# Latent attention: maxima and exponentials of opposite row halves sent to TensorE in turn, head groups in order 0,1,2,3

## The reference

```python
x + attn(xn) + ffn(xn)
# attn: 16 heads of width 8 within chunks of 16 tokens, once on the tokens in order,
#       once on every third token; both outputs summed, then a linear layer
# ffn:  y = xn + mla(rmsnorm(xn));  y + moe(rmsnorm(y))
# mla:
scores = einsum("bqhd,bkhd->bhqk", qq, kk) / sqrt(8)      # 16 heads of width 8, half of it rotated
probs  = softmax(where(tril(ones(S, S)), scores, min))    # causal, S = 512
y      = einsum("bhqk,bkhd->bqhd", probs, v) @ W_o
# moe:  one shared expert and 2 of 7 routed ones per token; all 8 are computed for every token
```

## Time and profile before

| | us |
|---|---|
| median of 3 runs | 514.09 |
| lowest and highest | 512.26, 516.3 |
| the profiled execution, its own time | 514.96 |
| its span, first to last instruction | 513.0 |
| mean granted TensorE clock | 0.963 of full |
| TensorE busy | 464.1 (90%) |
| VectorE busy | 361.0 (70%) |
| ScalarE busy | 265.1 (52%) |

### The profile page before, as it was taken

One profiled execution on the slowest core, in us unless ns is written; L12 is line 12 of the kernel. 1 busy time (PEld: TensorE's weight loads), 2 busy tenths in 40 slices (PEclk: granted clock), 3 DMA queues, 4 the chain that ended last, 5 costly groups with the idle time before them and its releaser, 6 DMA issues.

```text
span 513.0 us, 11641 instructions
## 1 busy us (share of the span) xinstructions
PE 464.1 (90%) x4428; PEld 244.8 (48%) x4428; DVE 361.0 (70%) x1049; ACT 265.1 (52%) x486; POOL 53.2 (10%) x52
## 2 busy tenths in 40 slices
PE   3774988999999999999999997999999999987995
PEld 2322343445453555545455554454545545654652
DVE  6463586687767877776577784666677775688886
ACT  6252447457766554877754385776543444212110
POOL 4231001141001121010002120000010000010000
PEclk9868699999999999999999997999999999999899
DMA  6156000156000227100001264000400000000000
GB/s 206 24 137 116 0 3 2 21 127 134 3 2 3 65 56 134 27 3 2 2 3 34 54 125 68 1 3 2 125 1 4 2 1 22 0 22 1 1 20 21
DMA packets 18198, 20.22 MB, mean 39 GB/s; under 512 B 2824, under 2 KB 16392, under 8 KB 17352
## 3 DMA queue, kind: packets, MB, share of 16 engines
q1 hardware_dynamic: 18144, 19.49, 17.4%
HBM read 10.84 MB, written 7.47 MB: 36 GB/s over the span
## 4 chain that ended last, share of the span: by engine, by line
PE 60%; DVE 20%; DMA 6%; issue 5%; ACT 5%; SPq 3%; POOL 1%; DVEq 0%; ACTq 0%; POOLq 0%
PE bank_A L1080 7%; PE bank_c L1043 6%; PE bank_A L1001 6%; PE bank_B L1026 6%; PE bank_M L1091 6%; DVE x L942 4%; PE bank_B L1124 4%; DMA q_stack<-in_c_rows 4%; PE bank_M L1098 4%; DVE k_diag L922 3%; PE bank_B L1031 3%; PE bank_M L985 3%; DVE k_diag L927 3%; PE bank_A L1130 2%; SPq L478 2%
## 5 line engine op out<-in xcount | busy, mean ns | idle before, releaser
L672 ACT ACTIVATE p_mla<-bank_B 128x512 f32<-128x512 f32 (+1 forms) x176 | 97.5, 561 | 92.9 <-PE bank_B L1031 91.4
L819 DVE CUSTOM_DVE_ANT_0 differences<-masks,bank_A 128x384 bf16<-128x384 bf16 (+1 forms) x128 | 78.4, 613 | 25.2 <-PE bank_A L1001 20.2
L651 ACT ACTIVATE pT_loc<-sT_loc 32x512 f32<-32x512 f32 x136 | 85.1, 625 | 4.8 <-DVE sT_loc L845 3.4
L1001 PE MATMUL bank_A<-k_stack,q_stack 50*128 50x128 bf16 (+3 forms) x256 | 65.2, 307 | 11.0 <-DMA q_stack<-in_c_rows 7.4
L1124 PE MATMUL bank_B<-xrT,k_diag 128*128 128x512 f32 x128 | 64.4, 617 | 3.9 <-DVE k_diag L922 3.2
L1026 PE MATMUL bank_B<-q_stack,k_stack 50*128 50x512 bf16 (+3 forms) x256 | 63.9, 302 | 0.6 <-DVE k_diag L922 0.2
L838 DVE TENSOR_REDUCE row_max<-bank_A 128x16 f32<-128x512 f32 (+1 forms) x36 | 24.8, 690 | 40.7 <-PE bank_A L1080 40.6
L1080 PE MATMUL bank_A<-k_diag,qT 128*32 128x512 f32 x272 | 50.5, 772 | 0.0
L1031 PE MATMUL bank_B<-masks 64*128 64x64 bf16 (+1 forms) x512 | 50.3, 202 | 0.0
L1043 PE MATMUL bank_c<-p_mla,v_mla 128*9 128x128 f32 (+3 forms) x512 | 47.5, 442 | 0.4 <-ACT p_mla L672 0.3
L1031 PEld LDWEIGHTS bank_B<-masks 64*128 64x128 bf16 x512 | 39.8, 95 | 14.3 <-issue 0.2
(11 more groups left out here) (135 smaller groups left out, 593.3 us busy)
## 6 DMA issues: line engine op xcount, KB each, us to landing
parts_dram<-parts SPq DMA_DIRECT2D x16, 192.0 KB, 2.7
k_stack<-parts_dram SPq DMA_DIRECT2D x8, 384.0 KB
q_stack<-parts_dram SPq DMA_DIRECT2D x8, 384.0 KB
parts_dram<-parts SPq DMA_DIRECT2D x16, 128.0 KB, 2.7
k_diag<-kT SPq DMA_DIRECT2D x64, 18.0 KB
x<-in_x SPq DMA_DIRECT2D x4, 256.0 KB, 6.6
parts_dram<-parts SPq DMA_DIRECT2D x16, 64.0 KB, 2.3
out<-x SPq DMA_DIRECT2D x4, 256.0 KB, 2.2
```

The costliest lines, as they stand in the source:

```text
L651: last = nc.scalar.activation(pT_loc[rows, :, rows], sT_loc[rows, t % 2, :].rearrange("p (h k) -> p h k", h=H), ACT.Exp, scale=SCALE)
L672: drained_by(nc.scalar.activation(p_mla[:, n % P_RING, m:m + len(heads), j * P:], src, ACT.Exp, scale=SCALE), step)
L819: drained_by(nc.vector.tensor_tensor_reduce(differences[:, 0:w], masked16[:, S - w:], bank[:, 0:w], -1.0, -NEG, ALU.add, ALU.min, dst), step)
L1001: last = nc.tensor.matmul(bank[:, n * w:(n + 1) * w], q_stack[b % 2][rows, h % 8, i * P:(i + 1) * P], k_stack[b % 2][rows, h % 8, 0:w], st ...
```

## The change

`GROUP_ORDER` becomes 0, 1, 2, 3. The lists "maxima" and "latent" of all batches give way to one list "scores" from key -0.29 to 4.0, made of 18 slots of 11 elements (`LEAD` = 2). In slot n an element holds an S step of group n (counted through all batches) and the E step of the same place of group n-2, then what is due behind it (PV of the key block that has just ended; SHIFT of the group before, behind the second element). The first two slots hold S alone, the last two E alone. An element is placed as a whole, so nothing stands between its S and its E. The units of S come in the order i = 3, 2, 1, 0, which gives the two steps of an element equal numbers of matmuls of equal width. TensorE issues such a pair in turn: first matmul of E, first of S, second of E, second of S, and then the masks of E with those of S in turn, where S has any. The stretches of the outputs and of the norm of batches 1 and 2 move slightly. No operation is added or removed on any engine.

```diff
@@ -77,14 +77,15 @@
 LOCAL_TILES = S // P
 
 
-GROUP_ORDER = [0, 2, 1, 3]
+GROUP_ORDER = [0, 1, 2, 3]
+LEAD = 2
 
 
 def score_units():
 
     units = []
     for g in GROUP_ORDER:
-        for i in range(NT):
+        for i in reversed(range(NT)):
             n = S // ((i + 1) * P)
             units += [(i, list(range(h, min(h + n, 4 * g + 4)))) for h in range(4 * g, 4 * g + 4, n)]
     return units
@@ -103,14 +104,13 @@
 
 
 SPREAD = {
-    "latent": [(0, 1.12), (1.12, 2.02), (2.02, 2.86), (2.86, 4)],
-    "maxima": [(-0.29, 0.63), (0.61, 1.44), (1.56, 2.46), (2.49, 3.54)],
+    "scores": [(-0.29, 4.0)],
     "local": [(-0.53, 0.39), (0.36, 1.22), (1.34, 2.21), (2.28, 3.15)],
     "project": [(0.01, 0.29), (0.35, 1.13), (1.49, 2.32)],
     "stacks": [(-0.37, -0.37), (0.48, 0.48), (1.3, 1.3), (2.29, 2.29)],
     "values": [(-1.27, -1.27), (0.38, 0.38), (1.36, 1.36), (2.34, 2.34)],
-    "outputs": [(1.18, 1.34), (2.12, 2.26), (2.86, 2.97), (4.02, 4.27)],
-    "norm": [(1.31, 1.53), (2.33, 2.54), (3.17, 3.65), (4.28, 4.57)],
+    "outputs": [(1.18, 1.34), (2.13, 2.26), (3.08, 3.19), (4.02, 4.27)],
+    "norm": [(1.31, 1.53), (2.33, 2.54), (3.26, 3.65), (4.28, 4.57)],
     "experts": [(3.17, 5.49)],
     "statistics": [(-0.41, -0.41)],
 }
@@ -120,7 +120,7 @@
 
     keyed = [(lo + (hi - lo) * (k + 0.5) / len(one), n, k, step)
              for n, (one, lo, hi) in enumerate(parts) for k, step in enumerate(one)]
-    return [x[3] for x in sorted(keyed, key=lambda x: x[:3])]
+    return [step for x in sorted(keyed, key=lambda x: x[:3]) for step in (x[3] if isinstance(x[3], list) else [x[3]])]
 
 
 def plan():
@@ -129,20 +129,27 @@
         return [("LN", b), ("XT", b, 0), ("LK", b), ("LQ", b), ("XT", b, 1), ("MA", b, 0), ("MB", b, 0),
                 ("MA", b, 1), ("MB", b, 1)]
 
-    def maxima(b):
-        steps = []
-        for n, g in enumerate(GROUP_ORDER):
-            steps += [("S", b, u) for u in range(PER_GROUP * n, PER_GROUP * n + PER_GROUP)] + [("SHIFT", b, g)]
-        return steps
-
-    def latent(b):
-        steps, late = [], []
-        for g in GROUP_ORDER:
-            for j in range(NT):
-                units = [("E", b, g, j, u) for u in range(len(exp_units(g, j)))]
-                steps += units[:1] + late + units[1:]
-                late = [("PV", b, g, j)]
-        return steps + late
+    def scores():
+
+
+        groups = [(b, g) for b in range(B) for g in GROUP_ORDER]
+        found, shift, late = [], [], []
+        for n in range(len(groups) + LEAD):
+            here = groups[n] if n < len(groups) else None
+            back = groups[n - LEAD] if n >= LEAD else None
+            exps = [("E",) + back + (j, u) for j in range(NT) for u in range(len(exp_units(back[1], j)))] if back else []
+            for k in range(PER_GROUP):
+                unit = []
+                if here:
+                    unit.append(("S", here[0], PER_GROUP * GROUP_ORDER.index(here[1]) + k))
+                if back:
+                    unit.append(exps[k])
+                found.append(unit + late + (shift if k == 1 else []))
+                late = []
+                if back and (k + 1 == PER_GROUP or exps[k + 1][3] != exps[k][3]):
+                    late = [("PV",) + exps[k][1:4]]
+            shift = [("SHIFT",) + here] if here else []
+        return found + [late]
 
     def outputs(b):
         return [("Y", b, i) for i in range(NT)] + [("YT", b), ("X1", b)]
@@ -173,9 +180,9 @@
     steps = first[:4] + [("KD", 0), ("WF",)] + first[4:]
     at = SPREAD
 
-    lists = [(experts(range(B)), *at["experts"][0])]
+    lists = [(experts(range(B)), *at["experts"][0]), (scores(), *at["scores"][0])]
     for b in range(B):
-        lists += [(latent(b), *at["latent"][b]), (maxima(b), *at["maxima"][b]), (local(b), *at["local"][b]),
+        lists += [(local(b), *at["local"][b]),
                   (outputs(b), *at["outputs"][b]), (norm(b), *at["norm"][b]), ([("ST", b)], *at["stacks"][b]),
                   ([("MV", b)], *at["values"][b])]
     for b in range(1, B):
@@ -259,6 +266,8 @@
     gu_no, down_no = numbers(steps, {"GU"}), numbers(steps, {"DOWN"})
     single = [step for step in steps if step[0] == "S" and UNITS[step[2]][0] >= 2]
     downs = [step for step in steps if step[0] == "DOWN"]
+    beside = {e: s for s, e in zip(steps, steps[1:]) if (s[0], e[0]) == ("S", "E")}
+    waits_for_e = set(beside.values())
 
     with ExitStack() as ctx:
         def sb(name, shape, dt=F32):
@@ -950,6 +959,41 @@
             pe.wait_ge(set_up, 1)
             pe.wait_ge(eye_in, 16)
 
+            def half_of(h):
+                return slice(SLOT * (h // 8), SLOT * (h // 8) + SLOT)
+
+            def maxima_matmul(step, n):
+                b, (i, heads) = step[1], UNITS[step[2]]
+                h, w = heads[n], (i + 1) * P
+                rows = slice(half_of(h).start, half_of(h).start + STACK_ROWS)
+                return nc.tensor.matmul(bank_of(step)[:, n * w:(n + 1) * w],
+                                        q_stack[b % 2][rows, h % 8, i * P:(i + 1) * P],
+                                        k_stack[b % 2][rows, h % 8, 0:w], start=n == 0, stop=i >= 2,
+                                        skip_group_check=True)
+
+            def maxima_mask(step, n, low):
+                i, heads = UNITS[step[2]]
+                w = (i + 1) * P
+                return nc.tensor.matmul(bank_of(step)[:, (n + 1) * w - P + low * SLOT:(n + 1) * w],
+                                        half_eye[half_of(heads[n]), low, :],
+                                        half_causal[half_of(heads[n]), low, low * SLOT:], start=False, stop=True,
+                                        skip_group_check=True)
+
+            def exp_matmul(step, m):
+                _, b, g, j, u = step
+                h, w = exp_units(g, j)[u][m], S - j * P
+                rows = slice(half_of(h).start, half_of(h).start + STACK_ROWS)
+                nc.tensor.matmul(bank_of(step)[:, m * w:(m + 1) * w], k_stack[b % 2][rows, h % 8, j * P:(j + 1) * P],
+                                 q_stack[b % 2][rows, h % 8, j * P:], start=m == 0, stop=False, skip_group_check=True)
+
+            def exp_mask(step, m, low):
+                _, b, g, j, u = step
+                w = S - j * P
+                return nc.tensor.matmul(bank_of(step)[:, m * w:m * w + SLOT * (low + 1)],
+                                        half_eye[half_of(4 * g), low, :],
+                                        half_causalT[half_of(4 * g), low, 0:SLOT * (low + 1)],
+                                        start=False, stop=True, skip_group_check=True)
+
             for _ in range(6):
                 nc.tensor.matmul(bank_c[:, 0:P], eye[:], eye[:], start=True, stop=True)
             for step in steps:
@@ -990,25 +1034,17 @@
                                                 start=True, stop=True)
                     full_by(last, step)
                 elif kind == "S":
-                    i, heads = UNITS[step[2]]
-                    w = (i + 1) * P
                     if step[2] == 0:
                         pe.wait_ge(k_ones_in[b % 2], 16 * 2)
                         pe.wait_ge(stacks_in, STACK_IN * (b + 1))
-                    half_rows = slice(SLOT * (heads[0] // 8), SLOT * (heads[0] // 8) + SLOT)
-                    rows = slice(half_rows.start, half_rows.start + STACK_ROWS)
-                    for n, h in enumerate(heads):
-                        last = nc.tensor.matmul(bank[:, n * w:(n + 1) * w],
-                                                q_stack[b % 2][rows, h % 8, i * P:(i + 1) * P],
-                                                k_stack[b % 2][rows, h % 8, 0:w], start=n == 0, stop=i >= 2,
-                                                skip_group_check=True)
-                    for n in range(len(heads) if i < 2 else 0):
-                        for low in range(2):
-                            c = (n + 1) * w - P + low * SLOT
-                            last = nc.tensor.matmul(bank[:, c:(n + 1) * w], half_eye[half_rows, low, :],
-                                                    half_causal[half_rows, low, low * SLOT:], start=False, stop=True,
-                                                    skip_group_check=True)
-                    full_by(last, step)
+                    if step not in waits_for_e:
+                        for n in range(len(UNITS[step[2]][1])):
+                            last = maxima_matmul(step, n)
+                        if UNITS[step[2]][0] < 2:
+                            for n in range(len(UNITS[step[2]][1])):
+                                for low in range(2):
+                                    last = maxima_mask(step, n, low)
+                        full_by(last, step)
                 elif kind == "SHIFT":
                     g = step[2]
                     wait_drained(pe, ("S", b, PER_GROUP * (GROUP_ORDER.index(g) + 1) - 1))
@@ -1017,21 +1053,23 @@
```

(24 more changed lines are left out.)

## The result

The changed kernel takes 550.6 us (median of 4 runs, 545.8 to 553.5) against 515.2; the ratio is 1.067, 95% interval 1.057 to 1.078. The forecast was 487.

What follows compares the result with a forecast made beforehand. TensorE's instruction stream from 75 to 437 us was taken as the bound. Scores 33 us shorter, less 2, times 0.83 gives 26, plus 2.6 from loads makes 28; 514.96 - 28 = 487 us, range 480 to 494.

Steps and rivals of the forecast that it cites:

- The masks: Small mask matmuls of j=2 and j=3 pairs, two halves in turn: 2.5 us lost, if 0.030 us per start were the floor 4.5.
- The stream: TensorE's score steps: 84 us with pairs overlapped in opposite row halves, against 117 before, 33 us less.
- the 2.6 us for the loads: The wait of 2.58 us at 315.57 us, where S of the last batch waits for its loads, is gone.
- the masks or the order would not overlap at all: Two rivals: masks not overlapped, 524 us; no overlap from the order at all, 520 us; chance 0.09 together.
- (9): From 75 to 437 us TensorE's stream gets some 31 us shorter; 0.83 comes through, as VectorE only rises to 78%.
- (5): E starts 18 us later, so some 10 E steps move to a fuller stretch: costs 0 to 3 us, taken as 2.
- (8): E now also waits for the bank of its S before either starts: price nothing to 3 us.
- (7): SHIFT issued two pairs into the next group; SP's queue holds nothing that waits later than before: cost nothing.
- (2): Reversed i matches S and E in columns and number of matmuls, so a pair costs its E: 49.6 us paired.
- The clock: Around no change, chance 0.05: late loads or a lower granted clock somewhere in the new order eat the gain.
- TensorE waits for VectorE's banks of ring A by tens of us: Sign that would show the forecast wrong: TensorE held up by tens of us for the PSUM banks that S uses.
- VectorE or the hand-over takes half: Rival: VectorE's load or the two-bank rings let only half of the 31 us through, 499 us; chance 0.20.

Runs made afterwards that it cites:

- same_half: The changed kernel with group order 0,2,1,3, so both steps of a pair lie in the same row half and can't overlap: 585.5 us, ratio 1.141.
- unalternated: The changed kernel with its list as it is, but TensorE issues all matmuls of S, then all of E: 551.9 us, ratio 1.065.
- a3b2: The changed kernel with three PSUM banks in ring A (S, local scores) and two in ring B (E): 533.6 us, ratio 1.036.
- short_max_after: The changed kernel with VectorE's maxima of i=2 and i=3 taken over the last 128 columns alone: 530.1 us, ratio 1.027.
- gapped: The changed kernel with the slots of its single list following the old stretches of S, with gaps between them: 538.9 us, ratio 1.036.
- stretch_e: Kernel before with group order 0,1,2,3 and i reversed, plus E, PV, outputs and norm in the change's stretches: 523.3 us, ratio 1.017.
- experts_later: The changed kernel with the experts' list starting at key 3.45 instead of 3.17, its end as before: 539.0 us, ratio 1.046.
- scores_early: The changed kernel with the scores' list ending at key 3.8 instead of 4.0, outputs moved with it: 540.8 us, ratio 1.047.
- stretch_s: Kernel before with group order 0,1,2,3 and i reversed, plus S steps in the change's uniform stretches, E staying: 542.1 us, ratio 1.053.
- reversed_alone: The kernel before with i from 3 to 0 and nothing else, group order left at 0,2,1,3: 525.4 us, ratio 1.016.
- order_alone: The kernel before with its lists kept, only group order 0,1,2,3 and i from 3 to 0: 512.2 us, ratio 0.986.

## Why the prediction was wrong

**Right.** The cost of steps and runs (176 runs of half-array steps, 175 forecast). The overlap of opposite halves in all four kinds of pairs. The masks: forecast 2.5 us of loss, measured none, 0.021 us per start. The stream: 33 us shorter by forecast, about 40 by the account above. Also right: the 2.6 us for the loads, gone. Of the rivals, that the masks or the order would not overlap at all can be dropped; so can the sum's upper bound from weight loads one behind the other.

**The step that failed is (9), with (5) and (8) under it:** that of 31 us of shorter stream 0.83 comes through, because VectorE was at 71% and TensorE had hardly a wait. It took the few waits of the kernel before as a property of the engines' loads. They were a property of the list. The new list, at an equal stream, costs 70 us (same_half against before). I priced the new list's placement of S and E against all other work at 2 us (5), and a late bank at 0 to 3 (8); measured, TensorE's waits for p_mla, neg_max, scratch and shift rose from 8 to 44 us. And the last 12 us of shorter stream, those of the alternation, brought 1.3 (unalternated against the change).

How the list does it, as far as the runs show: S without gaps meets VectorE's blocks (the 4.2 us wait behind PICK; a3b2, short_max_after and gapped each give 12 to 20 us back); E late and dense beside the experts (stretch_e 11 us, experts_later 12, scores_early 10). No run relieves ScalarE, whose p_mla is the longest cause of waits (10.3 us, 12.9 in a3b2); its part stays open. In (7) I held that nothing in SP's queue could delay a SHIFT; a SHIFT does stand behind the stacks' loads for 10 us, and for 6.2 already in the kernel before. It decides nothing in the change, only in stretch_s.

**A second failed step: the reversal of i at nothing** (2). I looked only at how sizes match on TensorE. In the old lists it costs 8 us, by a lower clock at equal work and equal idle time; in the new list, nothing that can be measured. Why the clock falls is open.

**The clock** was in the forecast, together with late loads, as a risk of 5 in 100, and by the account it takes 30 us. Mostly it goes with waits: TensorE idles, the clock falls to 1.2 GHz, and the steps behind the wait run slower too. From 212 to 222 us the changed kernel runs at 1.2 GHz throughout, after waits of 0.65 and 1.05 us that end at 209.7 and 211.8 us:

```profile
212.00:222.00 10.00, 9.53 (x52) 4.27 (x52) 4.18 (x11) 5.04 (x10) 0.00 (x0) 0.50 0.01 3
```

But reversed_alone has such a stretch of 20 us with hardly a wait before it, so waits are not the whole of it. Where the forecast named a sign of error, "TensorE waits for VectorE's banks of ring A by tens of us", it was that sign that came (26 us for neg_max and scratch), and so did the other, a clock below 0.9 in the middle (0.80 from 200 to 225 us).

**The rival that was nearest**, "VectorE or the hand-over takes half", had the mechanism and too small a price: I let the hand-over take half of the gain. It can take more than all of it, since moving 352 steps also moves them out of the order that the old stretches gave them. The page "TensorEngine Tiling (Array Packing)" of the Trainium skill, section PSUM Bottleneck, says that after a faster array the copies out of PSUM may bind. Here a3b2 and short_max_after bear that out (17 and 20 us), though not as a bound by load: VectorE was busy 65% of the span.

**The order of issue.** The page "TensorE: Matmul & The Clock Gate" of the Trainium skill, Part 3 (The mechanism), says that matmuls start in program order. The traces agree in part. In unalternated the first E matmul of the i=0 and j=3 pair starts at 139.14 us with three masks of S still to start, but with nearly all of S behind it, and the pair takes 1.08 us instead of 0.67. So for steps of one matmul the order is worth nothing, as the overlap in the earlier trace rows had it, and for steps of several it is worth 0.23 to 0.41 us a pair. In time none of it came through.

**Open.** The account splits the 36 us into clock and idle time, but the runs don't say how much of the clock's 30 us would go if the waits went. The parts don't add either (30 + 11 from S and E on top of order_alone, some 17 of them the SHIFT alone, against 38 between order_alone and the change with its further overlap). What gluing S, E, PV and SHIFT costs is not known.
